# Routing on logits in PSUM, and places of rows summed by TensorE, in a macaron transformer block

## The chip, the cores and the metric

The kernel runs on one core of one Trainium2 chip. The metric is the device time of one execution in microseconds (us); it is the median of several executions. Engines: TensorE (PE, matmuls; PEld is its weight load), VectorE (DVE), ScalarE (ACT), GpSimd (POOL) and SyncE (SP, which issues DMAs). SBUF is the working memory; PSUM is eight banks that TensorE writes and VectorE and ScalarE read and write.

## The reference

The input x is 8 sequences of 512 rows of 128 values. The block applies a mixture of experts, then attention, then the same mixture of experts again:

```python
x = x + 0.5 * ffn(layernorm(x))          # 8 experts, 2 per row
x = x + attn(layernorm(x))               # 16 heads of 64, one shared K and V, causal, position bias
x = x + 0.5 * ffn(layernorm(x))

def ffn(x):
    gates = softmax(x @ gate_w)                    # 8 logits a row
    top_v, top_i = top_k(gates, 2)
    top_v = top_v / sum(top_v)
    h = gelu(einsum('nd,edf->enf', xt, fc_w))      # 128 -> 512
    eo = einsum('enf,efd->end', h, proj_w)         # 512 -> 128
    return sum(top_v * eo at top_i)                # the two chosen experts
```

## The kernel before

The 4096 rows are 32 tiles of 128. The kernel sends each row only to its two experts: it chooses the experts, gives each pair of row and expert a place in the list of that expert, scatters the rows there, and runs 71 tiles of sorted rows through the experts' matrices. This happens twice. The first expert stage runs from the start to about 250 us. The attention follows, to about 841 us. The second expert stage begins at about 865 us.

The routing of the second stage is woven into the attention. Its rows come in six groups of tiles (`GROUPS`: 8, 8, 8, 4, 2 and 2 tiles), as soon as the attention has finished them. A group is cut into pieces of up to four tiles (`PIECES`), so the first three groups have two pieces and the others one. The tasks of group i are:

- V2, A2, I2, X2: mean and deviation, and the normalised rows in `slot`.
- T2, C2, L2 (TensorE, ScalarE, TensorE), one for each piece: rows transposed, copied to SBUF, and multiplied with the gate; the logits stand in a PSUM bank, 8 columns a tile.
- G2 (VectorE, L1207), one for each piece: the logits are copied from the bank to `lga` in SBUF, and the bank is free.
- H2 (VectorE, L1217 to L1228), two halves, for the first and the second expert: the maximum, an `is_equal` with it, a product with `rev8` that favours the lower expert, a maximum, and an `is_equal` that leaves a one-hot `hot2`; the first half ends with the chosen logit masked in `lgb`, the second with `wt2` (L1226) and the sum of both one-hots, `hot2b` (L1227). `hot2_done` (L1228) follows.
- P2 (TensorE, L1505 and L1506): `hot2b` times all ones (rows of each tile by expert) and times `before` (rows ahead of this one in its tile), into one bank.
- W2 (ScalarE) and W3 (VectorE, L1231 to L1233): the weights.
- B2 (VectorE), two halves. The first (L1240 to L1250) runs a scan over tiles in `scan2` in SBUF, one step for each shift of 1, 2 and 4, adds the running counts `run`, and frees the bank by `base2_done`. The second (L1253 to L1255) picks each pair's place.
- SC (GpSimd, L795): the scatters.

The attention's own tasks, of batch b and step n (16 steps, 4 query tiles in each of 4 groups of heads): Q, K and V products; S, scores of four heads into two banks; TTR (VectorE, L1302), bias and maximum; EXP (ScalarE, L967); R (L1309) and N (GpSimd, L805), the normalisation, two instructions on SBUF each; T (TensorE, L1549) and TC (VectorE L1315 or ScalarE L974), transposed probabilities; AV, O, Y and YA (VectorE, L1324), the output.

All of these are put in order at build time by a list planner (`attention_order`). Each task has a cost, needs, a kind of bank that it takes and the task that frees this bank, and a due time (`wanted_at`); an engine takes the ready task that is due first. The engines then run their lists in that order, and wait on semaphores. There are four "front" banks for Q, K, V, xT, T2, L2, P2 and S; S takes two.

After the last group VectorE makes the lists of the second stage (`second_lists`), and SyncE loads sorted rows once all scatters have landed.

## Time and profile before

| | us |
|---|---|
| median of 3 runs | 1031.23 |
| lowest and highest | 1029.57, 1034.24 |
| profiled execution | 1030.17 |
| its span | 1028.4 |

| engine | busy us | share | instructions |
|---|---|---|---|
| PE | 936.7 | 91% | 7811 |
| PEld | 772.0 | 75% | 7811 |
| DVE | 763.2 | 74% | 2860 |
| ACT | 640.4 | 62% | 1765 |
| POOL | 637.2 | 62% | 613 |

How to read what follows. The profile records one execution. A timeline row gives start, duration, engine, source line, operation, the tile written and those read (buffer numbers left out, so `bank` is any PSUM bank), shapes, and in brackets how long the engine stood idle before it and what it waited for. A waits row gives who waited for whom: us in total, times, longest. A grouped row gives the busy time and the mean in ns. A windows row gives for one stretch its length, then busy time and instructions of PE, PEld, DVE, ACT and POOL, the granted TensorE clock as a share of 2.4 GHz, the DMA engines' share and GB/s.

### The profile page before, as it was taken

The numbers are of one execution on the slowest core, as the hardware profiler recorded it, in microseconds if no ns is written. First come the engines' busy times: TensorE is split into PE (matmuls) and PEld (weight loads), VectorE is DVE, ScalarE is ACT, GpSimd is POOL, SyncE is SP. The second block draws the span as 40 slices with busy tenths as digits, with TensorE's granted clock in tenths as the row PEclk, the third lists the DMA queues.
The fourth block names the chain that finished last, engine by engine and source line by source line (L and its number), as shares of the span: only waits on it lengthen the run. The fifth ranks groups of instructions, "written<-read, shape, count | busy, mean of one in ns | idle before, by whom it ended". The sixth has DMA issues, their size and how long they took to land.

```text
span 1028.4 us, 25473 instructions
## 1 busy us (share of the span) xinstructions
PE 936.7 (91%) x7811; PEld 772.0 (75%) x7811; DVE 763.2 (74%) x2860; ACT 640.4 (62%) x1765; POOL 637.2 (62%) x613
## 2 busy tenths in 40 slices
PE   8599999989999998899999899999899973999990
PEld 8499999957776777677776677777676753999990
DVE  7676456588788789877888877678978856777774
ACT  4735234488787888787888777788678651333330
POOL 2357577299889788788545587545586543555551
PEclk8699999999999999999999999999999995999996
DMA  9422556525556550010000000000010021222227
GB/s 270 132 65 68 91 128 150 107 61 127 133 104 135 119 109 15 19 33 2 2 2 1 12 33 2 2 2 1 12 33 1 5 88 54 74 68 72 71 58 245
DMA packets 86514, 69.57 MB, mean 68 GB/s; under 512 B 8034, under 2 KB 76388, under 8 KB 86384
## 3 DMA queue, kind: packets, MB, share of 16 engines
q1 hardware_dynamic: 77120, 48.92, 19.5%
q0 software_dynamic: 9264, 19.03, 7.3%
q8 instruction: 68, 1.11, 0.5%
q14 instruction: 62, 0.51, 0.2%
HBM read 32.07 MB, written 36.31 MB: 66 GB/s over the span
## 4 chain that ended last, share of the span: by engine, by line
PE 76%; DVE 9%; issue 4%; ACT 4%; DMA 3%; POOL 2%; SPq 1%; DVEq 0%; POOLq 0%; ACTq 0%
PE bank L1549 13%; PE bank L1540 13%; PE bank L1565 12%; PE bank L1601 12%; PE bank L1611 11%; PE bank L1572 6%; PE bank L1425 2%; PE bank L1427 2%; PE bank L1426 2%; PE bank L1593 2%; DMA xr<-xn_dram,gidx 1%; ACT prob L967 1%; DVE pT L1315 1%; DMA which<-y_dram 1%; DVE lnt L1044 1%
## 5 line engine op out<-in xcount | busy, mean ns | idle before, releaser
L805 POOL TENSOR_TENSOR prob<-prob,rsum 128x256 f32<-128x256 f32 (+3 forms) x256 | 314.0, 1254 | 138.4 <-DVE rsum L1309 137.7
L967 ACT ACTIVATE prob<-prob,negmax 128x384 f32<-128x384 f32 (+3 forms) x512 | 282.1, 553 | 66.9 <-DVE negmax L1302 66.2
L1302 DVE CUSTOM_DVE_ANT_0 prob<-bank,bias_tab 128x384 f32<-128x384 f32 (+3 forms) x512 | 229.1, 484 | 60.3 <-PE bank L1540 58.0
L904 ACT ACTIVATE hT<-bank 128x512 f32<-128x512 f32 x149 | 89.0, 597 | 205.9 <-PE bank L1601 205.9
L1549 PE MATMUL bank<-ident,prob 128*128 128x128 f32 x1280 | 186.5, 280 | 6.3 <-DVE pT L1315 5.2
L1540 PE MATMUL bank<-kst,qst 64*128 64x256 f32 (+2 forms) x1536 | 165.8, 343 | 14.0 <-DVE negmax L1302 7.6
L1549 PEld LDWEIGHTS bank<-ident,prob 128*128 128x128 f32 x1280 | 145.0, 142 | 39.4 <-issue 23.0
L1565 PE MATMUL bank<-pT,vst 128*64 128x256 f32 x1280 | 162.5, 389 | 1.3 <-DVE x_sb L1324 1.0
L1601 PE MATMUL bank<-xrT,w1t 128*128 128x128 f32 x1192 | 161.9, 280 | 1.0 <-DVE xrT L1360 0.9
L1540 PEld LDWEIGHTS bank<-kst,qst 64*128 64x128 f32 x1536 | 112.2, 186 | 62.5 <-issue 40.6
L1611 PE MATMUL bank<-w_sb,hT 128*128 x1192 | 158.7, 277 | 0.0
L1601 PEld LDWEIGHTS bank<-xrT,w1t 128*128 128x128 f32 x1192 | 148.5, 196 | 2.7 <-DVE xrT L1360 2.2
L1611 PEld LDWEIGHTS bank<-w_sb,hT 128*128 128x128 f32 x1192 | 146.5, 194 | 0.1
L1315 DVE COPY pT<-bank 128x512 f32<-128x512 f32 x181 | 123.6, 686 | 27.2 <-PE bank L1549 25.3
L818 POOL DMA_INDIRECT xr<-xn_dram,gidx x78 | 78.2, 1002 | 73.4 <-PE bank L1593 43.4
L1565 PEld LDWEIGHTS bank<-pT,vst 128*64 128x64 f32 x1280 | 82.8, 137 | 53.5 <-issue 20.1
L831 POOL DMA_INDIRECT y_dram<-yo,sidx x71 | 70.1, 987 | 75.2 <-DVE sidx L1358 68.2
L1372 DVE COPY w1t<-w_sb 128x512 f32 x149 | 66.4, 446 | 62.2 <-PE bank L1601 52.5
L967 ACT ACTIVATION_READ_ACCUMULATOR prob<-prob,negmax 128x1 f32 x512 | 96.8, 189 | 0.0
L974 ACT ACTIVATE pT<-bank 128x512 f32<-128x512 f32 x139 | 81.2, 588 | 24.9 <-PE bank L1549 24.1
L795 POOL DMA_INDIRECT slot_dram<-slot,idx x64 | 62.6, 979 | 35.0 <-DVE idx L1255 19.0
L1572 PE MATMUL bank<-wo_sb,ot 128*128 128x128 f32 x512 | 82.4, 288 | 1.8 <-ACT ot L980 1.7
(233 smaller groups left out, 1192.1 us busy)
## 6 DMA issues: line engine op xcount, KB each, us to landing
slot_dram<-fill SPq DMA_DIRECT2D x15, 990.0 KB, 7.2
y_dram<-yo SPq DMA_DIRECT2D x78, 64.0 KB
xr<-slot_dram SPq DMA_DIRECT2D x71, 66.0 KB, 1.8
w_sb<-L_ffn_fc_w SPq DMA_DIRECT2D x2, 2048.0 KB, 10.2
bias_tab<-bias_dram SPq DMA_DIRECT2D x8, 512.0 KB
slot_dram<-fill SPq DMA_DIRECT2D x2, 1056.0 KB, 7.5
x_sb<-L_attn_x SPq DMA_DIRECT2D x4, 512.0 KB, 5.6
xn_dram<-xn SPq DMA_DIRECT2D x4, 512.0 KB, 3.8
```

The lines of the kernel that those rows point to most:

```text
L805: g.tensor_tensor(out=pv, in0=pv, in1=rsum[:, n % 8, hs].unsqueeze(2).to_broadcast([P, 2, (n % QT + 1) * P]), op=ALU.mult).then_inc(norm_d ...
L904: a.activation(hT[:, n % 2, :], bank[2 + n % 2][:], ACT.Gelu).then_inc(gelu_done, 1)
L967: a.activation(prob[n % 8][:, h, :], prob[n % 8][:, h, :], ACT.Exp, scale=-1.0, bias=negmax[:, i % 8:i % 8 + 1], accum_out=lsum[:, n % 8, ...
L974: a.activation(pT[:, (b * NB + blk(n, jj)) % RING, :], BANK_OF["T", b, n, jj][:], ACT.Copy).then_inc(pt_act, 1)
L1302: v.tensor_tensor_reduce(out=prob[n % 8][:, h, :], in0=BANK_OF["S", b, n, c0][h % 2][:, at:at + w], in1=bias_tab[:, HG * (n // QT) + h, SE ...
L1315: v.tensor_copy(pT[:, (b * NB + blk(n, jj)) % RING, :], BANK_OF["T", b, n, jj][:]).then_inc(pt_dve, 1)
L1540: ins = t_.matmul(out[o][:, at:at + w], qst[rows, g % 2, zq, c, t * P:(t + 1) * P], kst[rows, b % 2, zk, 0:w], start=(i == 0), stop=(i == 2))
L1549: ins = t_.transpose(out[:, h * P:(h + 1) * P], prob[n % 8][:, h, jj * P:(jj + 1) * P], ident[:])
L1565: ins = t_.matmul(BACK_BANK[n % 2][o * DH:(o + 1) * DH, 0:2 * P], vst[:, b % 2, jj, :], heads, start=(jj == 0), stop=(jj == n % QT))
L1572: ins = t_.matmul(BACK_BANK[n % 2][:, 2 * P:2 * P + D], ot[:, n % 2, c * P:(c + 1) * P], wo_sb[:, n // QT, c, :], start=(c == 0), stop=(c ...
L1601: ins = t_.matmul(bank[2 + n % 2][:, c * P:(c + 1) * P], w1t[:, n % 2, c * P:(c + 1) * P], xrT[:, n % 2, :], start=True, stop=True)
L1611: ins = t_.matmul(bank[6 + n % 2][:, 0:D], hT[:, n % 2, c * P:(c + 1) * P], w2_sb[:, ds(e, 1), c, :].rearrange("p a d -> p (a d)"), start= ...
```

## The change

Three things.

- The last piece of each group has no G2. Its logits stay in their PSUM bank, at the place of their tile in the group, and the logits of an earlier piece are copied from `lga` into the same bank. `rev8` is copied there too. H2 works on these; the masked logits go to columns 128 and up of this bank, and `lgb` is gone. The bank is free when H2's second half is done.
- P2 multiplies `hot2b`, with one more tile of zeros behind it, with `before`, and adds for each tile q of the group one product with ones into the columns of all later tiles. The columns then hold the rows ahead of each row in the whole group, and the last tile's columns the group's totals. That is one matmul per tile and one more, where there were two.
- B2's first half is two additions (`run` to the bank's numbers, the totals to `run`), with its result in the bank. `scan2` and `base2_done` are gone. The bank is freed by B2's second half.

The planner's costs and the tasks that free the banks change with that, so the attention is put in order anew.

```diff
-                    task(("G2", m), {"dve": 0.2}, [("L2", m), ("H2", i - 1, 1)], None, ("L2", m))
-                task(("H2", i, 0), {"dve": 1.2}, [("G2", m) for m in mine] + [("B2", i - 1, 1), ("W3", i - 1)])
-                task(("H2", i, 1), {"dve": 1.6}, [("H2", i, 0)])
+                    if m != mine[-1]:
+                        task(("G2", m), {"dve": 0.2}, [("L2", m), ("H2", i - 1, 1)], None, ("L2", m))
+                task(("H2", i, 0), {"dve": 1.4}, [("G2", m) for m in mine[:-1]] + [("L2", mine[-1]), ("B2", i - 1, 1), ("W3", i - 1)])
+                task(("H2", i, 1), {"dve": 1.6}, [("H2", i, 0)], None, ("L2", mine[-1]))
...
-                task(("P2", i), {"pe": 0.3}, [("H2", i, 1)], "front")
-                task(("B2", i, 0), {"dve": 1.5}, [("P2", i)], None, ("P2", i))
-                task(("B2", i, 1), {"dve": 1.2}, [("B2", i, 0)])
+                task(("P2", i), {"pe": 0.3 + 0.1 * len(group)}, [("H2", i, 1)], "front")
+                task(("B2", i, 0), {"dve": 0.5}, [("P2", i)])
+                task(("B2", i, 1), {"dve": 1.2}, [("B2", i, 0)], None, ("P2", i))
...
                         if c == 0:
-                            dve.wait_ge(logit2_sb, max(LOGIT2_SB["G2", m] for m, piece in enumerate(PIECES) if piece[0] in group))
+                            if b == 0:
+                                async_done(v.memset(hot2b[:, 2 * QT, :], 0.0))
+                            dve.wait_ge(logit2_ps, LOGIT2_PS["L2", mine[-1]])
+                            if mine[:-1]:
+                                dve.wait_ge(logit2_sb, max(LOGIT2_SB["G2", m] for m in mine[:-1]))
+                                ahead_of_last = slice(js.start, js.start + sum(len(PIECES[m]) for m in mine[:-1]))
+                                async_done(v.tensor_copy(room[:, 0:(ahead_of_last.stop - js.start) * E], lga[:, ahead_of_last, :].rearrange("p t e -> p (t e)")))
+                            step_done(v.tensor_copy(room[:, 2 * QT * E:2 * QT * E + E], rev8[:]))
...
-                        rev = rev8[:].unsqueeze(1).to_broadcast([P, nt, E])
-                        src = (lga, lgb)[c]
+                        rev = room[:, 2 * QT * E:2 * QT * E + E].unsqueeze(1).to_broadcast([P, nt, E])
+                        src = (logits, rest)[c]
...
-                            step_done(v.scalar_tensor_tensor(out=lgb[:, js, :], in0=hot2[:, 0, js, :], scalar=MASKED, in1=lga[:, js, :],
+                            step_done(v.scalar_tensor_tensor(out=rest, in0=hot2[:, 0, js, :], scalar=MASKED, in1=logits,
                                                              op0=ALU.mult, op1=ALU.add))
...
                             dve.wait_ge(prefix2_ps, b + 1)
-                            async_done(v.memset(scan2[:, :, 0:4, :], 0.0))
-                            async_done(v.tensor_copy(scan2[:, 0, 4, :], run[:]))
-                            step_done(v.tensor_copy(scan2[:, 0, 5:4 + nt, :], tot[:, 0:nt - 1, :]))
-                            cur = 0
-                            for sh in [x for x in (1, 2, 4) if x < nt]:
-                                step_done(v.tensor_tensor(scan2[:, 1 - cur, 4:4 + nt, :], scan2[:, cur, 4:4 + nt, :],
-                                                          scan2[:, cur, 4 - sh:4 + nt - sh, :], ALU.add))
-                                cur = 1 - cur
-                            async_done(v.tensor_tensor(run[:], scan2[:, cur, 3 + nt, :], tot[:, nt - 1, :], ALU.add))
-                            step_done(v.tensor_tensor(lgb[:, js, :], scan2[:, cur, 4:4 + nt, :], pre, ALU.add))
-                            v.engine_nop().then_inc(base2_done, 1)
+                            step_done(v.tensor_tensor(place2, rows_ahead, run[:].unsqueeze(1).to_broadcast([P, nt, E]), ALU.add))
+                            async_done(v.tensor_tensor(run[:], sums[:, nt * E:(nt + 1) * E], run[:], ALU.add))
...
-                                step_done(v.tensor_tensor(eqa[:, js, :], lgb[:, js, :], hot2[:, c, js, :], ALU.mult))
+                                step_done(v.tensor_tensor(eqa[:, js, :], place2, hot2[:, c, js, :], ALU.mult))
...
-                        hot = hot2b[:, slots_of(GROUPS[b]), :].rearrange("p t e -> p (t e)")
-                        t_.matmul(out[:, 0:nt * E], ones_bf[:], hot, start=True, stop=True)
-                        t_.matmul(out[:, 2 * QT * E:(2 * QT + nt) * E], before[:], hot, start=True, stop=True).then_inc(prefix2_ps, 1)
+                        hot = hot2b[:, 2 * QT - nt:2 * QT + 1, :]
+                        t_.matmul(out[:, 0:(nt + 1) * E], before[:], hot.rearrange("p t e -> p (t e)"), start=True, stop=False)
+                        for q in range(nt):
+                            ins = t_.matmul(out[:, (q + 1) * E:(nt + 1) * E], ones_bf[:], hot[:, q:q + 1, :].to_broadcast([P, nt - q, E]),
+                                            start=False, stop=(q == nt - 1))
+                        ins.then_inc(prefix2_ps, 1)
```

## Rows read from the trace of the kernel before

**Rows 1.** The page, busy time: engine, us, share of the span, instructions.
```profile
PE 936.7 (91%) x7811; PEld 772.0 (75%) x7811; DVE 763.2 (74%) x2860; ACT 640.4 (62%) x1765; POOL 637.2 (62%) x613
```

**Rows 2.** Busy time by stretch: attention with routing, then the handover to the experts.
```profile
250.00:836.00 586.00, 564.40 (x4639) 419.82 (x4641) 468.19 (x1677) 459.42 (x1351) 410.68 (x364) 0.99 0.16 37
836.00:865.20 29.20, 7.75 (x52) 5.23 (x48) 18.70 (x100) 8.02 (x15) 9.14 (x9) 0.65 0.29 98
```

**Rows 3.** Waits of TensorE from 245 to 845 us: us in total, times, longest.
```profile
PE bank L1540 <- DVE negmax L1302: 5.8, 4, 2.6
...
PE bank L1540 <- DVEq L1250: 2.8, 2, 1.4
...
PE bank L1505 <- DVEq L1228: 2.6, 1, 2.6
```

**Rows 4.** Timeline, H2 of group 0: start, us, engine, instruction, idle before it.
```profile
412.73 3.74 POOL L805 TENSOR_TENSOR prob<-prob,rsum 128x1024 f32<-128x1024 f32 x2 [1.47 <-DVE rsum L1309]
...
412.79 1.92 DVE L1218 TENSOR_TENSOR eqa<-lgb,top 128x64 f32<-128x64 f32 x1
...
414.74 1.82 DVE L1219 TENSOR_TENSOR eqa<-eqa,rev 128x64 f32<-128x64 f32 x1
...
417.61 0.19 PE L1505 MATMUL bank<-hot2b,ones_bf 128*128 128x64 bf16 x1 [2.58 <-DVEq L1228]
```

**Rows 5.** Timeline, an instruction with one input in a bank beside GpSimd's.
```profile
423.42 2.04 POOL L805 TENSOR_TENSOR prob<-prob,rsum 128x512 f32<-128x512 f32 x2 [1.69 <-DVE rsum L1309]
...
424.18 0.68 DVE L1281 TENSOR_TENSOR xTl<-bank,xTh 128x512 fp32r<-128x512 f32 x1
```

**Rows 6.** Groups of VectorE instructions by shape: busy us, mean ns, idle before.
```profile
L1253 DVE TENSOR_TENSOR eqa<-lgb,hot 128x64 f32<-128x64 f32 x6 | 3.4, 562 | 0.1
...
L1221 DVE TENSOR_TENSOR hot<-rev,slot 128x64 f32<-128x64 f32 x3 | 0.7, 226 | 0.1
...
L1245 DVE TENSOR_TENSOR scan<-scan 128x16 f32<-128x16 f32 x2 | 0.3, 174 | 0.1
...
L1249 DVE TENSOR_TENSOR lgb<-scan,bank 128x16 f32<-128x16 f32 x2 | 0.3, 162 | 0.0
```

**Rows 7.** Timeline, the sums of group 1 and the S behind them.
```profile
574.48 0.11 DVE L1240 MEMSET scan<- 128x64 f32 x1
...
574.76 1.35 DVE L1245 TENSOR_TENSOR scan<-scan 128x64 f32<-128x64 f32 x3
...
576.23 0.21 DVE L1249 TENSOR_TENSOR lgb<-scan,bank 128x64 f32<-128x64 f32 x1
...
576.64 0.79 PE L1540 MATMUL bank<-kst,qst 64*128 64x384 f32 x6 [1.41 <-DVEq L1250]
```

**Rows 8.** Timeline, the sums of group 3 and the AV behind them.
```profile
815.65 0.58 DVE L1241 COPY scan<-run 128x8 f32<-128x8 f32 x1
...
817.61 1.08 PE L1565 MATMUL bank<-pT,vst 128*64 128x256 f32 x8 [0.98 <-DVE x_sb L1324]
```

**Rows 9.** Timeline, eight bf16 matmuls in a row in the first routing.
```profile
29.47 0.45 PE L1480 MATMUL bank<-which,in_tile 128*128 128x40 bf16 x8 [3.79 <-DVE in_tile L1131]
```

**Rows 10.** Busy time by stretch, behind P2's wait in group 0; clock third from last.
```profile
418.30:421.70 3.40, 3.40 (x18) 2.87 (x17) 2.44 (x14) 2.66 (x10) 2.94 (x4) 0.50 0.07 19
421.70:425.10 3.40, 3.40 (x29) 2.55 (x28) 3.13 (x15) 2.06 (x6) 1.71 (x3) 1.00 0.09 24
```

**Rows 11.** Timeline of the handover: sums of group 5, scatters, first expert tile.
```profile
853.89 0.11 DVE L1240 MEMSET scan<- 128x64 f32 x1
...
854.67 0.17 DVE L1253 TENSOR_TENSOR eqa<-lgb,hot 128x16 f32<-128x16 f32 x1
...
855.94 0.96 POOL L795 DMA_INDIRECT slot_dram<-slot,idx  x1 [1.79 <-DVE idx L1255]
...
865.22 0.48 PE L1593 MATMUL bank<-ident,xr 128*128 128x128 f32 x1 [11.78 <-DMA xr<-slot_dram]
```

**Rows 12.** Timeline, G2 of group 0's last piece, then the S that takes its bank.
```profile
405.98 0.19 DVE L1207 COPY lga<-bank 128x32 f32<-128x32 f32 x1
...
407.81 0.96 PE L1540 MATMUL bank<-kst,qst 64*128 64x512 f32 x6
```

32 lines of the change are left out of this document (20 added, 12 removed).

## The prediction

> **What bounds the kernel now.** I read the busy line first, then busy time by stage, then TensorE's waits, then the timeline around each wait that bears on the changed code. The page gives TensorE 91% of the span [rows 1]. By stage [rows 2]: from 250 to 836 us, the attention with the second routing woven in, TensorE is busy 564.40 of 586.00 us, so 21.6 us of idleness is all that a faster VectorE could hand back there; VectorE is busy 468.19, so it has 118 us of slack. From 836.0 to 865.2 TensorE has next to nothing to do: that is a chain of small steps, and each step that goes shortens the run. From 865.2 on the experts run, and the change touches nothing there. So the change can act on (1) those TensorE waits of the attention that the routing causes, (2) the chain at the handover, (3) TensorE's own work.
>
> Of (1), the waits show three kinds [rows 3]: P2 waited 2.6 us once for `hot2_done` (L1228), S waited 2.8 us in two places for `base2_done` (L1250, the bank of the sums), and S waited 5.8 us for L1302, the ordinary traffic of the attention.
>
> Why the routing is late is seen at group 0 [rows 4]. GpSimd's normalisation (L805, two instructions in 3.74 us) starts at 412.73. VectorE's L1218 starts at 412.79 and takes 1.92 us, L1219 then 1.82 us, each ending just as one GpSimd instruction ends. The same shape undisturbed takes about 0.23 us (L1221 in [rows 6]), so 1.92 + 1.82 - 0.45 = 3.3 us are waiting, and P2 left TensorE idle for 2.58 us. What waits has two inputs in SBUF. With one in PSUM it does not: L1281, started at 424.18 under GpSimd's instructions of 423.42 to 425.46, took its usual 0.68 us [rows 5].
>
> The Trainium skill says the same (SBUF: State Buffer, section Who interferes with whom): a VectorE instruction with two SBUF inputs is blocked by a GpSimd one that reads SBUF, whichever starts second. By that rule L1226 (two slices of `top2`) and L1227 (two slices of `hot2`) stay exposed after the change; that is rival B.
>
> **The change part by part**, against the profiled execution's 1030.17 us.
>
> *H2, group 0.* L1217 to L1223 get a PSUM input or have one SBUF input already; only the chain of L1226 and L1227 can still wait. Without the 3.3 us, `hot2_done` comes before P2's place in TensorE's order, and 2.58 us go; if GpSimd's second instruction holds L1227 instead, some 1 us goes; if both positions fall badly, nothing. I take -1.7, ends 0 and -2.6. Right behind this gap TensorE ran at 1.2 GHz for 3.40 us [rows 10], starting 18 matmuls there against 29 in the next 3.40 us at 2.4 GHz: 3.4 x (1 - 18/29) = 1.3 us lost. If the idleness before it shrinks, this may go too: -0.6, ends 0 and -1.3.
>
> *B2, groups 1 and 2* (one wait for L1250 each, 2.8 us in all [rows 3]). The sums start at 574.48; three scan steps take 1.35 us, two of them behind GpSimd, and S waited 1.41 us for the bank until 576.64 [rows 7]. The change leaves two instructions (0.21 + 0.08, with 0.03 to 0.04 between: about 0.33 us) but hands the bank back only after B2's second half, five instructions at about 0.25 us, 1.2 us. That is 1.5 us where there were 1.96 (574.48 to 576.44, the end of L1249): the wait shrinks by 0.5 us, not by 1.4. -1.0 for both, ends 0 and -2.8. B2's second half gains too: six L1253 took 562 ns on average, against 226 for the shape undisturbed (L1221), 2.0 us in all [rows 6], and S waits for VectorE 5.8 us in the stage [rows 3]. I let 0.6 come through, ends 0 and -2.0.
>
> *B2, group 3.* L1241 stood 0.58 us behind GpSimd, and YA, next on VectorE behind the sums, let TensorE wait 0.98 us [rows 8]. The sums lose L1241 and all scan steps: -0.8, ends 0 and -1.0.
>
> *The handover.* Group 5, two tiles. G2 goes (0.17), the copy of `rev8` comes (0.17): nothing. The sums start at 853.89 and B2's second half at 854.67: 0.78 us, now 0.21 + 0.08 = 0.3. W3 still sets their start. GpSimd's last four scatters waited for exactly this index (idle 1.79 until 855.94), TensorE for what follows from them [rows 11]. Group 4's same saving is swallowed by the wait for group 5. So -0.46. Not shown by any row is a VectorE write into PSUM. The chain now has two of them per group (the `rev8` copy and the masked logits), four in all, each from the 0.17 us of the same write to SBUF to 0.23 us, the largest undisturbed VectorE row of this code; I take 0.17, since reads of PSUM are no dearer here: with one input in the bank L1249 takes 162 ns where L1245, both in SBUF, takes 174 [rows 6].
>
> A rule speaks against this step: the Trainium skill (VectorE: DVE Perf Modes, section on the TRN2 errata) puts the fixed part of a PSUM-source operation at 120 cycles against 58 from SBUF at 0.96 GHz, 65 ns more. Twenty operations on the handover's chain change their source (nine in each H2, two in B2), so its estimate is +1.3 us, and -0.46 would turn into +0.8. The 162 against 174 ns above contradict it, and I leave it out.
>
> *P2.* One matmul per tile and one more, where there were two: 7 more in three groups, 3 in one, 1 in two, 26 in all. Eight bf16 matmuls of 128x40 in a row took 0.45 us [rows 9]; with one at about 0.19 the next seven come 0.037 us apart. 26 x 0.037 = +0.96 us, nearly all in the full stage. Ends 0 (they fit into waits) and +2.6 (0.1 us each, the cost that the new listing gives its planner).
>
> *New holds.* The last L2 of a group now keeps one of the four front banks until H2 is through, and S needs two. By the order that the planner writes for the kernel before, in group 0 the copy at 405.98 freed the bank for the S at 407.81 [rows 12]; H2 ended only at 417.4 [rows 4]. In group 3 a Q took it at once. In groups 1 and 2 its taker, an S, started after the time at which H2 ended anyway: nothing. VectorE's waits on GpSimd that vanish shorten the hold, and transposes and AV fill TensorE meanwhile: I take +0.8 for groups 0 and 3 together, ends 0 and the slow rival. The remaining additions (the copy of `lga`, `rev8`, one memset, some 2 us in all) lie in VectorE's 118 us of slack.
>
> Sum: -1.7 - 0.6 - 1.0 - 0.6 - 0.8 - 0.46 + 0.96 + 0.8 = -3.4, or 1026.8. The median of the runs, 1031.23, stands 1.06 above the profiled execution, and I carry that over: 1027.8 us.
>
> **The rivals.**
>
> A, *everything comes back*: all terms at their good ends but P2's, -2.6 - 1.3 - 2.8 - 2.0 - 1.0 - 0.46 + 0.96 = -9.2, 1022.0 us. For it: every gap named ends at an instruction of the routing. Against: 21.6 us is the whole idleness, and the bank is handed back later.
>
> B, *the wait moves*: L1226, L1227 and W3 still read SBUF alone, GpSimd is busy 410.68 of 586 us [rows 2], and an H2 that runs faster to its end meets the instruction it used to outwait. Then only the sums are shorter, against 0.96 for P2: about 1031 us.
>
> C, *slower, by the held bank*: S in groups 0 and 3 cannot take its two banks until H2 is done, H2 is queued behind VectorE's other work because it is due later, and TensorE runs dry. Price: the largest wait of S in the attention is 2.6 us [rows 3]; with 1.3 us of lower clock behind it, 3.9, in two groups 7.8; with P2's 0.96 and half of the gains that remain left over, 1031.2 + 7.8 + 1.0 - 2.0 = 1038 us. It decides once H2 needs longer from the last L2 than S can be put off, in more than one group. Against: groups 1 and 2 pay nothing. For: since the order is planned anew, every later task shifts as well, and which of them meet a GpSimd instruction is drawn again; that shift has no sign and is in the width of the range.
>
> **How the numbers follow.** Forecast 0.45, with a range of its own from 1024.5 to 1031; A 0.17; B 0.20; C 0.18. About 0.5% (5.2 us) is what a measurement of this kernel can tell from no change: faster is below 1026.1, slower above 1036.4. Faster: A and a third of the forecast, 0.32. Slower: C, 0.18. Same: 0.50. The range takes in all but C: 1021.5 to 1035.5.
>
> **What would show it.** Right, if L1218, L1219 and L1253 of the new kernel take their 0.23 us under GpSimd's instructions; if P2 no longer waits; if the handover from the last L2 to the last scatter is 0.5 us shorter; if TensorE's idleness in the attention falls by 3 to 5 us and its work grows by 1. B shows as long instances of the wt and hot2b lines; C as new waits of S or Q for H2's last step. I am wrong if the new order of the attention moves more than the routing does: then gaps appear at L1302 and L1549, far from H2.

## The result, and the profile of the changed kernel

| | before | after |
|---|---|---|
| median, us | 1032.74 | 1019.04 |
| profiled execution, us | 1030.17 | 1018.65 |
| its span, us | 1028.4 | 1016.7 |

The changed kernel takes 0.9872 of the time before, with an interval of 0.9853 to 0.9891: 13 us faster. That is below the whole range of 1021.5 to 1035.5, and below the 1022.0 of the rival in which everything comes back. The direction was right, the size was not. The ratio leaves out one of the changed kernel's four executions, which took 1862.64 us; the others took 1018.47 to 1019.43.

The page after, busy time; it answers [rows 1].

```profile
PE 935.8 (92%) x7837; PEld 772.6 (76%) x7837; DVE 747.7 (74%) x2834; ACT 640.3 (63%) x1764; POOL 638.2 (63%) x613
```

TensorE has 26 instructions more, as the step on P2 counted, and the same busy time; VectorE has 15.5 us less. So nearly all of the time came out of idleness. Where, the busy time by stretch tells: around the batches that carry groups 0, 1 and 2, then nearly the whole attention with routing. First the kernel before (columns as in [rows 2]).

```profile
370.00:455.00 85.00, 79.43 (x649) 59.38 (x647) 72.20 (x257) 66.09 (x193) 67.17 (x63) 0.98 0.19 45
530.00:612.00 82.00, 77.55 (x633) 57.11 (x631) 67.27 (x236) 64.36 (x189) 50.84 (x46) 1.00 0.04 14
686.00:768.00 82.00, 77.54 (x637) 57.39 (x633) 67.86 (x240) 62.56 (x184) 50.87 (x45) 1.00 0.04 13
245.00:829.00 584.00, 562.40 (x4627) 417.98 (x4627) 468.85 (x1683) 460.83 (x1353) 409.30 (x363) 0.99 0.16 37
```

The same stretches of the changed kernel.

```profile
370.00:455.00 85.00, 81.83 (x689) 61.18 (x685) 69.68 (x263) 68.46 (x199) 70.19 (x66) 0.98 0.20 48
530.00:612.00 82.00, 80.33 (x671) 60.18 (x670) 66.34 (x247) 66.50 (x200) 56.28 (x50) 1.00 0.05 15
686.00:768.00 82.00, 80.35 (x673) 60.11 (x674) 66.15 (x242) 66.01 (x191) 55.94 (x50) 1.00 0.05 15
245.00:829.00 584.00, 571.60 (x4745) 426.56 (x4745) 461.58 (x1689) 467.02 (x1363) 416.82 (x369) 0.99 0.16 37
```

TensorE's idleness from 245 to 829 us falls from 584 - 562.40 = 21.6 us to 12.4. Each of the three stretches gives 2.4 to 2.8 us of it (2.40, 2.78, 2.81). The attention itself, from its first AV to its last, takes 614.7 us where it took 626.2: 11.5 us, the whole difference of the two profiled executions.

What TensorE still waits for in that stretch (columns as in [rows 3]).

```profile
PE bank L1561 <- DVE pT L1322: 5.6, 4, 1.4
PE bank L1552 <- DVE qst L1296: 2.8, 1, 2.8
PE bank L1552 <- DVE negmax L1309: 2.6, 1, 2.6
PE bank L1577 <- DVE x_sb L1331: 0.6, 3, 0.2
```

Of the routing's waits in [rows 3] none is left: `hot2_done` and `base2_done` are gone and no wait for H2's last step has taken their place. What B2 still causes is small: 0.2 us of an S that waits for a bank of the sums (`idx`, L1262, in group 3), and the 0.6 us of AV. (Lines have moved: S is L1552, T L1561, AV L1577, TTR L1309, TC L1322, YA L1331, GpSimd's normalisation L809.) H2 of group 0, which answers [rows 4]:

```profile
408.73 2.89 POOL L809 TENSOR_TENSOR prob<-prob,rsum 128x768 f32<-128x768 f32 x2 [1.49 <-DVE rsum L1316]
...
409.28 0.22 DVE L1234 TENSOR_TENSOR eqa<-bank,top 128x64 f32<-128x64 f32 x1
...
409.54 0.22 DVE L1235 TENSOR_TENSOR eqa<-eqa,bank 128x64 f32<-128x64 f32 x1
...
413.93 0.22 DVE L1243 TENSOR_TENSOR hot2b<-hot 128x64 bf16<-128x64 f32 x1
...
417.99 0.20 PE L1514 MATMUL bank<-hot2b,before 128*128 128x72 bf16 x1
```

These two steps are of H2's first half, and they take 0.22 us under GpSimd's normalisation. The steps of [rows 4] that took 1.92 and 1.82 us are of the second half. In the changed kernel that half runs at 412.57, when GpSimd issues gathers (`DMA_INDIRECT`, 411.77 to 416.51) and no normalisation is under way, so this group alone does not show what the bank did for it. The fair comparison is the first half with the same order of tasks and its operands in SBUF (`e13_sbuf_operands`, see the experiments):

```profile
408.09 2.89 POOL L810 TENSOR_TENSOR prob<-prob,rsum 128x768 f32<-128x768 f32 x2 [1.49 <-DVE rsum L1317]
...
408.57 1.07 DVE L1235 TENSOR_TENSOR eqa<-lga,top 128x64 f32<-128x64 f32 x1
...
409.67 1.39 DVE L1236 TENSOR_TENSOR eqa<-eqa,rev 128x64 f32<-128x64 f32 x1
...
412.71 0.96 PE L1553 MATMUL bank<-kst,qst 64*128 64x512 f32 x6 [1.25 <-DVE qst L1297]
```

1.07 and 1.39 us there, 0.22 and 0.22 with an operand in the bank, and TensorE's wait of 1.25 us for `qst`, the task behind them, is gone. Over the whole trace it is as clear. Take VectorE's two-input instructions of at most 64 columns that begin while a GpSimd `tensor_tensor` has 0.3 us or more still to run. In the kernel before there are 28, all with both inputs in SBUF, and all 28 take longer than 0.3 us. In the changed kernel the 12 with both in SBUF do, and the 18 with one in a bank do not.

In the changed kernel `hot2b` ends at 414.15, P2 comes in its turn at 417.99, and nothing waits. The sums of group 1, which answer [rows 7]:

```profile
569.03 6.89 POOL L809 TENSOR_TENSOR prob<-prob,rsum 128x1024 f32<-128x1024 f32 x6 [5.46 <-DVE rsum L1316]
...
573.29 0.22 DVE L1256 TENSOR_TENSOR bank<-bank,run 128x64 f32<-128x64 f32 x1
573.55 0.17 DVE L1257 TENSOR_TENSOR run<-bank,run 128x8 f32<-128x8 f32 x1
...
574.71 0.24 DVE L1262 CAST idx<-posa 128x16 int32<-128x16 f32 x1
...
575.76 1.08 PE L1577 MATMUL bank<-pT,vst 128*64 128x256 f32 x8 [0.20 <-DVE x_sb L1331]
```

All seven instructions of B2 are done in 1.66 us (573.29 to 574.95) below a GpSimd chain, where the first half alone took 1.96 and the second another 1.94. TensorE loses 0.20 us to what follows them.

The handover, which answers [rows 11].

```profile
843.18 0.17 DVE L1256 TENSOR_TENSOR bank<-bank,run 128x16 f32<-128x16 f32 x1
...
843.47 0.16 DVE L1260 TENSOR_TENSOR eqa<-bank,hot 128x16 f32<-128x16 f32 x1
...
844.73 0.96 POOL L799 DMA_INDIRECT slot_dram<-slot,idx  x1 [1.83 <-DVE idx L1262]
...
853.98 0.48 PE L1605 MATMUL bank<-ident,xr 128*128 128x128 f32 x1 [11.34 <-DMA xr<-slot_dram]
```

The sums take 0.29 us (843.18 to 843.47) where they took 0.78. From the last group of AV products to this first matmul of the experts it is 853.98 - 827.49 = 26.49 us, against 865.22 - 838.26 = 26.96 before: 0.47 us shorter.

### The profile page after: what moved, and what is told of

The parts are those of the page before. It is cut to its first block, busy times and chain, and to the rows that moved or that the text cites. A ratio compares the mean times of both kernels' runs of the same rounds, so it can differ in the third digit from the quotient of the medians.

```text
span 1016.7 us, 25497 instructions
## 1 busy us (share of the span) xinstructions
PE 935.8 (92%) x7837; PEld 772.6 (76%) x7837; DVE 747.7 (74%) x2834; ACT 640.3 (63%) x1764; POOL 638.2 (63%) x613
## 4 chain that ended last, share of the span: by engine, by line
PE 79%; DVE 8%; issue 4%; ACT 3%; DMA 3%; POOL 2%; SPq 1%; DVEq 0%; POOLq 0%; ACTq 0%
PE bank L1561 13%; PE bank L1552 13%; PE bank L1577 13%; PE bank L1613 12%; PE bank L1623 12%; PE bank L1584 6%; PE bank L1432 2%; PE bank L1434 2%; PE bank L1433 2%; ACT prob L971 2%; PE bank L1605 2%; DMA xr<-xn_dram,gidx 1%; DMA which<-y_dram 1%; DVE lnt L1048 1%; PE bank L1508 1%
## 5 line engine op out<-in xcount | busy, mean ns | idle before, releaser
L809 POOL TENSOR_TENSOR prob<-prob,rsum 128x256 f32<-128x256 f32 (+3 forms) x256 | 314.1, 1255 | 129.7 <-DVE rsum L1316 129.1
L1309 DVE CUSTOM_DVE_ANT_0 prob<-bank,bias_tab 128x384 f32<-128x384 f32 (+3 forms) x512 | 229.8, 484 | 64.5 <-PE bank L1552 61.8
L1561 PE MATMUL bank<-ident,prob 128*128 128x128 f32 x1280 | 184.0, 279 | 6.6 <-DVE pT L1322 5.6
L1552 PE MATMUL bank<-kst,qst 64*128 64x256 f32 (+2 forms) x1536 | 165.9, 343 | 7.9 <-DVE negmax L1309 4.5
L1561 PEld LDWEIGHTS bank<-ident,prob 128*128 128x128 f32 x1280 | 144.3, 142 | 37.0 <-issue 19.7
L1577 PE MATMUL bank<-pT,vst 128*64 128x256 f32 x1280 | 163.0, 390 | 0.8 <-DVE x_sb L1331 0.6
L1552 PEld LDWEIGHTS bank<-kst,qst 64*128 64x128 f32 x1536 | 112.6, 187 | 56.1 <-issue 38.8
L1322 DVE COPY pT<-bank 128x512 f32<-128x512 f32 x182 | 124.3, 686 | 27.2 <-PE bank L1561 25.6
L1577 PEld LDWEIGHTS bank<-pT,vst 128*64 128x64 f32 x1280 | 83.4, 137 | 52.8 <-issue 20.9
```

Source lines behind the costliest of these rows:

```text
L809: g.tensor_tensor(out=pv, in0=pv, in1=rsum[:, n % 8, hs].unsqueeze(2).to_broadcast([P, 2, (n % QT + 1) * P]), op=ALU.mult).then_inc(norm_d ...
L1309: v.tensor_tensor_reduce(out=prob[n % 8][:, h, :], in0=BANK_OF["S", b, n, c0][h % 2][:, at:at + w], in1=bias_tab[:, HG * (n // QT) + h, SE ...
L1322: v.tensor_copy(pT[:, (b * NB + blk(n, jj)) % RING, :], BANK_OF["T", b, n, jj][:]).then_inc(pt_dve, 1)
L1552: ins = t_.matmul(out[o][:, at:at + w], qst[rows, g % 2, zq, c, t * P:(t + 1) * P], kst[rows, b % 2, zk, 0:w], start=(i == 0), stop=(i == 2))
L1561: ins = t_.transpose(out[:, h * P:(h + 1) * P], prob[n % 8][:, h, jj * P:(jj + 1) * P], ident[:])
L1577: ins = t_.matmul(BACK_BANK[n % 2][o * DH:(o + 1) * DH, 0:2 * P], vst[:, b % 2, jj, :], heads, start=(jj == 0), stop=(jj == n % QT))
```

## The experiments

Two things for reading them. The chips differ: on two of them the kernel before took 1077 and 1089 us, on the others 1031 to 1033, so each ratio is against the kernel before on the same chip, and absolute times are compared on one chip alone. And "choice" is H2, "sums" is P2 with B2's first half, "place" is the tile that the second half of B2 reads.

### The whole change again, and one part alone, each with an order of its own

`e8_changed_again` and `e16_changed_third` are the changed kernel itself, beside the other experiments of their chip.

> The changed kernel itself, timed beside the others. The first four experiments ran on a chip on which the kernel before took 1077 us instead of 1032, so the changed kernel is needed as a reference on the same chip. If its gain does not depend on the chip: 12 to 14 us below the kernel before, a ratio of 0.987.

> The changed kernel, as reference for the other three on their chip. On a chip on which the kernel before takes 1032 us: 1018 us. On one on which it takes 1077 to 1089 us, where TensorE waits twice as long in the attention for other reasons: a ratio between 0.984 and 0.99.

Measured: 0.986 (0.9842 to 0.9877) and 0.9892 (0.9873 to 0.9911). The three ratios of the change, 0.9872 among them, scatter by 0.3%; differences below that between experiments on different chips say nothing.

`e1_sbuf_operands` and `e9_sbuf_operands`: the changed kernel with its order, P2 and B2, but with every operand back in SBUF.

```diff
-                        logits, rest = of_group(0), of_group(4 * QT * E)
+                        logits, rest = lga[:, js, :], lgb[:, js, :]
...
-                        rev = room[:, 2 * QT * E:2 * QT * E + E].unsqueeze(1).to_broadcast([P, nt, E])
+                        rev = rev8[:].unsqueeze(1).to_broadcast([P, nt, E])
...
-                        place2 = sums[:, 4 * QT * E:(4 * QT + nt) * E].rearrange("p (t e) -> p t e", e=E)
+                        place2 = lgb[:, js, :]
```

> The changed kernel with the same order of tasks on every engine, but the choice of experts works on copies in SBUF (lga, lgb, rev8) and the places are summed into SBUF. One copy per group (rev8) is left out. Only where the operands stand differs from the changed kernel. Theory 1 (the gain is VectorE no longer waiting for GpSimd): L1218, L1219 and L1253 of the old numbering are held again in some places, each by 0.8 to 1.9 us, and TensorE's gaps behind H2 and B2 come back: 5 to 9 us slower than the changed kernel, 1024 to 1028 us. Theory 2 (the gain is the newly planned order): within 1.5 us of the changed kernel, 1018 to 1020.5 us. Theory 3 (the gain is the shorter sums): within 1.5 us as well, since the sums keep their two instructions.

> The kernel of e1 once more (the changed kernel with its operands back in SBUF, order unchanged), now to be compared with the changed kernel's 1018.1 us and with the order-only kernel's 1033.2 us on a chip like theirs. Theory 1 (waits on GpSimd): between 1026 and 1029 us, with some VectorE instructions held 0.8 to 1.9 us. Theory 3 (shorter sums): at most 1020 us.

`e2_choice_only` and `e10_choice_only` have the new H2 with the old P2 and B2 (scan, `base2_done`), put in order anew (against the changed kernel):

```diff
-                task(("P2", i), {"pe": 0.3 + 0.1 * len(group)}, [("H2", i, 1)], "front")
-                task(("B2", i, 0), {"dve": 0.5}, [("P2", i)])
-                task(("B2", i, 1), {"dve": 1.2}, [("B2", i, 0)], None, ("P2", i))
+                task(("P2", i), {"pe": 0.3}, [("H2", i, 1)], "front")
+                task(("B2", i, 0), {"dve": 1.5}, [("P2", i)], None, ("P2", i))
+                task(("B2", i, 1), {"dve": 1.2}, [("B2", i, 0)])
```

> Only the first part of the change: the choice works in the bank of the logits, the bank is held until H2 is through; P2 and the scan in B2 are those of before. Theory 1: H2 no longer waits, P2's 2.6 us in group 0 and what follows go, but the scan steps of groups 1 and 2 can still be held: 1024 to 1028 us. Theory 2: unforeseeable, as the order is planned anew with other costs, 1018 to 1034 us. Theory 3: no gain, 1030 to 1034 us.

> The kernel of e2 once more (the choice in the bank, P2 and B2 as before). From e2's ratio of 0.998: 1029 us. If the choice alone gives the larger part on a chip without the other chip's additional waits: 1024 us.

`e3_places_only` and `e11_places_only` have the new P2 and B2 with the old H2 and G2, put in order anew (against the changed kernel):

```diff
-                    if m != mine[-1]:
-                        task(("G2", m), {"dve": 0.2}, [("L2", m), ("H2", i - 1, 1)], None, ("L2", m))
+                    task(("G2", m), {"dve": 0.2}, [("L2", m), ("H2", i - 1, 1)], None, ("L2", m))
```

> Only the second part of the change: TensorE sums the tiles ahead, B2 has two additions into the bank, and the bank is freed at B2's end; H2, G2 and their bank are those of before. Theory 3: the gaps of 1.4 us in groups 1 and 2 and of 1.0 in group 3 go, and 0.5 us at the handover: 1024 to 1027 us. Theory 1: half of the gain, since the product with the one-hots reads the bank now, but H2 is held as before with P2 behind it: 1026 to 1030 us.

> The kernel of e3 once more (the places in the bank and summed by TensorE, the choice as before). From e3's ratio of 0.9945: 1026 us. If choice and places add up to the whole 13.6 us: this one and e10 lie 13.6 us below twice the time before when taken together.

| | chip at 1077.11 | chip at 1089.47 |
|---|---|---|
| operands in SBUF | 0.9955 (0.9937 to 0.9973) | 0.9915 (0.9877 to 0.9953) |
| choice only | 0.9977 (0.996 to 0.9994) | 0.996 (0.9933 to 0.9987) |
| sums and place only | 0.9945 (0.9929 to 0.9962) | 0.9944 (0.9919 to 0.997) |

The kernel before took the times at the head of the table. Each part alone gains, the sums with the place about 0.55%, the choice 0.2 to 0.4%. Together that is 0.8 to 1%, under the 1.1 to 1.4% of the whole. But each had an order of its own, and the whole was not run on these two chips, so these runs cannot tell whether the parts help each other. Hence the third set.

### The held bank

`e4_held_bank` and `e12_held_bank`: the kernel before, with only the planner told that the last L2's bank is held until H2 is done, and the semaphores to match.

```diff
-                    task(("G2", m), {"dve": 0.2}, [("L2", m), ("H2", i - 1, 1)], None, ("L2", m))
+                    task(("G2", m), {"dve": 0.2}, [("L2", m), ("H2", i - 1, 1)], None, ("L2", m) if m != mine[-1] else None)
...
-                task(("H2", i, 1), {"dve": 1.6}, [("H2", i, 0)])
+                task(("H2", i, 1), {"dve": 1.6}, [("H2", i, 0)], None, ("L2", mine[-1]))
```

> The kernel before with one difference in the plan: the bank of the last logits of a group is freed by H2's second half instead of by the copy G2. No instruction differs, only the order and who waits for the bank. If the held bank costs what the prediction took: 0.8 us slower than before. Rival C of the prediction: up to 8 us slower. If it is free: no difference beyond 0.5 us, unless the order that is planned anew changes which VectorE instructions meet a GpSimd instruction, which by theory 2 can move the time by several us either way.

> The kernel of e4 once more (the kernel before, with the last logits' bank planned as held to the end of H2). From e4's ratio of 1.006: 1038 us. If its loss was a matter of the other chip: within 2 us of the kernel before. If the hold itself costs, TensorE's new gaps stand before an S or a Q that waits for H2; if it is the order planned anew, they stand elsewhere, behind VectorE instructions held by GpSimd.

Measured: 1.0063 (1.0046 to 1.008) and 1.002 (0.9991 to 1.005). A loss of 0.6% on the one chip, not to be told from nothing on the other. It doesn't come as the rival said. TensorE's waits in `e4_held_bank` show none for H2, one routing wait only, that for `base2_done` (L1252 here, 2.8 us in [rows 3]):

```profile
PE bank L1542 <- DVEq L1252: 4.5, 3, 1.6
```

The sums and the places have grown instead. Groups of VectorE instructions in `e4_held_bank`, columns as in [rows 6]:

```profile
L1247 DVE TENSOR_TENSOR scan<-scan 128x64 f32<-128x64 f32 x9 | 5.7, 632 | 0.3
L1255 DVE TENSOR_TENSOR eqa<-lgb,hot 128x64 f32<-128x64 f32 x6 | 4.6, 767 | 0.1
```

The scan steps took 360 ns on average before, the places 562 [rows 6]. In the new order the same instructions fall behind more of GpSimd's, while those of H2's second half, held before, are not. So the held bank itself shows no price; what changed is the order. That this order is what lost the 2 to 7 us (by the two ratios) is not shown: the kernel before has no trace on these two chips to set beside it.

### The same order for all: which part does it

These four run TensorE, VectorE, ScalarE and GpSimd in the order of the changed kernel; only the operands and instructions within the tasks differ. `e5_order_only` puts the old H2, P2 and B2 into it, with all operands in SBUF as in the first diff and the old sums:

```diff
-                            step_done(v.tensor_tensor(place2, rows_ahead, run[:].unsqueeze(1).to_broadcast([P, nt, E]), ALU.add))
-                            async_done(v.tensor_tensor(run[:], sums[:, nt * E:(nt + 1) * E], run[:], ALU.add))
+                            async_done(v.memset(scan2[:, :, 0:4, :], 0.0))
+                            async_done(v.tensor_copy(scan2[:, 0, 4, :], run[:]))
...
+                            step_done(v.tensor_tensor(lgb[:, js, :], scan2[:, cur, 4:4 + nt, :], pre, ALU.add))
```

> The order of tasks on every engine and the freeing of banks as in the changed kernel, but the instructions of the kernel before: the choice and the places in SBUF, the scan on VectorE, two products in P2. Theory 2 (the newly planned order gives the gain): within 2 us of the changed kernel. Theory 1 and theory 3 together (the instructions give it): at least as slow as the kernel before, ratio 0.998 to 1.005, since the planner also reckons with a B2 that is 1 us shorter than it is here. Compared with e1 (ratio 0.9955) it gives the worth of the shorter sums in one and the same order: theory 3 expects 2 to 4 us between them.

`e14_choice_in_bank_same_order` has the new H2 with those old sums.

> The order of the changed kernel and its choice in the bank, but P2 with two products and the scan in SBUF of the kernel before. Against e5 it has only the choice's operands moved. In the trace of e5 H2 was held 4.2 us in all and B2 4.4: 3 to 6 us faster than e5 and 8 to 11 us slower than the changed kernel.

`e13_sbuf_operands` has the new sums with all operands in SBUF (the first diff above).

> The order of the changed kernel, its P2 and its two additions in B2, but every operand of the choice and of the places in SBUF (as e1 and e9). If waiting on GpSimd is what costs: 8 to 10 us slower than the changed kernel, as in its trace 8.0 us of such waits stood in H2 and B2. If the shorter sums are what counts: within 2 us of the changed kernel.

`e15_places_in_sbuf` has everything but the place, which stands in SBUF:

```diff
-                        place2 = sums[:, 4 * QT * E:(4 * QT + nt) * E].rearrange("p (t e) -> p t e", e=E)
+                        place2 = lgb[:, js, :]
```

> The changed kernel with one operand elsewhere: the sum of rows ahead and run is written to SBUF instead of the bank, so that only the two products with the one-hots in B2's second half can wait for GpSimd. Such products were held 3 to 4 us in all in e13's order. If every us held here delays the bank for S: 3 to 5 us slower than the changed kernel; if they stand beside other work: within 1 us.

| in the order of the changed kernel | choice | sums | place | ratio | attention | idle | at 1.2 GHz |
|---|---|---|---|---|---|---|---|
| order only | SBUF | old | SBUF | 1.0015 (1.0 to 1.003) | 627.2 | 23.2 | 12.5 |
| choice in bank | bank | old | SBUF | 1.0006 (0.9989 to 1.0023) | 627.8 | 20.2 | 22.9 |
| operands in SBUF | SBUF | new | SBUF | 0.9949 (0.9929 to 0.9969) | 619.8 | 17.9 | 8.6 |
| place in SBUF | bank | new | SBUF | 0.9906 (0.9884 to 0.9928) | 616.7 | 15.0 | 9.2 |
| changed, same chip | bank | new | bank | 0.9892 (0.9873 to 0.9911) | 615.3 | 12.4 | 12.0 |

The last three columns are us of the traced execution, from the first AV to the last: its length, TensorE's idleness, and the time at 1.2 GHz. All but the first ran on one chip.

The new order brings nothing in time, if anything it costs 1.5 us. By time, the choice in a bank is worth 0.1% while the sums are long (across two chips, and below the 0.3% that says nothing there) and 0.4% (4.7 us) once they are short. The short sums are worth 0.7% with the choice in SBUF (across two chips again) and 1.1% (1032.28 to 1020.9, 11.4 us) with it in a bank. The place in a bank adds 0.9 us, less than the intervals. Operands in SBUF came out 5.5 us above the changed kernel, where 8 to 10 were expected if only the holds counted, and choice in bank 1.0 us below order only (across two chips), where 3 to 6 were.

By idleness the parts simply add up. The choice takes away 3.0 us with long sums and 2.9 with short ones, the short sums 5.3 and 5.2, the place 2.6. If there is more between the parts than that, it lies in the clock, see below.

What the sums and the place shorten is one wait of TensorE, that of AV for YA (`x_sb`). It stands, in this sequence, in the order only, choice in bank, operands in SBUF and place in SBUF kernels, from 245 to 829 us:

```profile
PE bank L1582 <- DVE x_sb L1339: 6.8, 3, 2.8
```
```profile
PE bank L1582 <- DVE x_sb L1339: 7.0, 3, 2.8
```
```profile
PE bank L1578 <- DVE x_sb L1332: 2.3, 2, 1.1
```
```profile
PE bank L1578 <- DVE x_sb L1332: 2.6, 3, 1.2
```

In the changed kernel it is the 0.6 us shown above. The choice does not touch it (6.8 and 7.0, 2.3 and 2.6 us). In the new order YA is queued on VectorE behind both halves of B2, so the whole of B2 now stands between TensorE and its next AV. In the choice in bank kernel, group 1:

```profile
576.68 0.11 DVE L1256 MEMSET scan<- 128x64 f32 x1
...
579.13 0.80 DVE L1268 TENSOR_TENSOR eqa<-lgb,hot 128x64 f32<-128x64 f32 x1
...
581.27 0.47 DVE L1339 TENSOR_TENSOR x_sb<-x_sb,bank 128x128 f32<-128x128 f32 x2
581.69 1.98 PE L1582 MATMUL bank<-pT,vst 128*64 128x256 f32 x8 [2.82 <-DVE x_sb L1339]
```

From the first instruction of B2 to YA it is 4.59 us here, 2.05 in the changed kernel (573.29 to 575.34). In the choice in bank kernel less idleness goes with more time at the lower clock. The first three stretches of the table above, in the choice in bank kernel:

```profile
370.00:455.00 85.00, 80.95 (x657) 60.32 (x656) 70.64 (x263) 68.33 (x198) 69.01 (x64) 0.98 0.21 48
530.00:612.00 82.00, 77.69 (x628) 58.07 (x625) 64.90 (x239) 62.94 (x188) 49.72 (x44) 0.96 0.04 13
686.00:768.00 82.00, 77.68 (x637) 58.26 (x636) 65.82 (x241) 61.98 (x184) 49.91 (x44) 0.98 0.04 13
```

A granted clock of 0.96 and 0.98 where the kernel before has 1.00: TensorE ran at 1.2 GHz for 22.9 us of the attention in all, against 12.5 in the order only kernel. It is idle 3.0 us less, but busy 3.6 us longer (627.8 - 20.2 against 627.2 - 23.2), and so the attention takes as long. The traced execution is no exception: over all ten the mean granted clock is 0.952 of full speed, against 0.955 over the ten of order only. Why more time at 1.2 GHz came with the shorter choice, no run shows.

What the place in SBUF costs is seen one instruction at a time. The operands in SBUF kernel, group 1, below GpSimd instructions from 570.96 to 577.84:

```profile
576.22 0.71 DVE L1261 TENSOR_TENSOR eqa<-lgb,hot 128x64 f32<-128x64 f32 x1
...
577.22 0.66 DVE L1263 CAST idx<-posa 128x16 int32<-128x16 f32 x1
...
578.69 1.08 PE L1578 MATMUL bank<-pT,vst 128*64 128x256 f32 x8 [1.12 <-DVE x_sb L1332]
```

Two instructions there are held for 0.5 us each. In the changed kernel the first reads a bank. The cast, the same instruction in both, took 0.24 us there, below GpSimd's chain too; why it escaped, no row shows.

### More products in P2

`e7_more_products`: the changed kernel with 32 more products of ones with the zero tile. They add nothing to the sums.

```diff
+                        for q in range(nt):
+                            ins = t_.matmul(out[:, (q + 1) * E:(nt + 1) * E], ones_bf[:], hot[:, nt:nt + 1, :].to_broadcast([P, nt - q, E]),
+                                            start=False, stop=(q == nt - 1))
```

> The changed kernel with one more product per tile in P2, of ones with the tile of zeros, 32 in all; same order, same result. It prices P2's matmuls in place. The prediction took 0.037 us for each: 1.2 us slower than the changed kernel. If they fit into waits: no difference (below 0.5 us). If each costs 0.1 us: 3.2 us slower.

Measured: 1019.86 us against 1018.07 for the changed kernel on the same chip, 1.8 us for 32, 0.056 us each; for the 26 of the change, 1.5 us. The intervals of the two overlap (0.9861 to 0.9895 and 0.9842 to 0.9877), so this is a rough size. The timeline has less for them, eight in 0.21 us (420.35 to 420.56):

```profile
420.35 0.35 PE L1516 MATMUL bank<-hot2b,ones_bf 128*128 128x64 bf16 x8
...
420.56 0.35 PE L1519 MATMUL bank<-hot2b,ones_bf 128*128 128x64 bf16 x8
```

That would be 0.026 us each, 0.8 us for 32. The other 1.0 us is small beside the scatter, and whether the products delay something else is open.

### The gaps that are left: the deviation

TensorE's six waits above 1 us that the changed kernel keeps (11.0 us in all, nearly all of the list of waits above) stand behind LN or I2, the tasks that compute the deviation. One of the largest, in the timeline:

```profile
331.09 4.27 DVE L1282 SCALAR_TENSOR_TENSOR shift<-mv,rstd 128x4 f32<-128x4 f32 x1
...
331.58 3.75 POOL L809 TENSOR_TENSOR prob<-prob,rsum 128x1024 f32<-128x1024 f32 x2
...
336.60 0.79 PE L1552 MATMUL bank<-kst,qst 64*128 64x384 f32 x6 [2.62 <-DVE negmax L1309]
```

An instruction on four columns, 0.16 us when it is alone, is held until 335.36, as GpSimd's two end at 335.33, and TensorE idles 2.62 us. `e6_deviation_in_bank` is the changed kernel with one operand of each of these steps in a PSUM bank (LN and I2 take a front bank for it, so the order is planned anew):

```diff
-                task(("LN", b), {"dve": 1.0}, [("LA", b)])
+                task(("LN", b), {"dve": 1.2}, [("LA", b)], "front", ("LN", b))
...
+                y, z = BANK_OF[k][:, 0:n], BANK_OF[k][:, 64:64 + n]
+                step_done(v.reciprocal(y, lnt[:, 4, own]))
+                async_done(v.scalar_tensor_tensor(out=z, in0=mean[:, own], scalar=-1.0, in1=y, op0=ALU.mult, op1=ALU.mult))
+                step_done(v.scalar_tensor_tensor(out=lnt[:, 0, own], in0=var[:, own], scalar=EPS, in1=y, op0=ALU.add, op1=ALU.mult))
+                step_done(v.scalar_tensor_tensor(out=lnt[:, 1, own], in0=lnt[:, 0, own], scalar=-0.5, in1=y, op0=ALU.mult, op1=ALU.mult))
```

> The changed kernel, and the same idea carried on to the deviations (LN and I2): the reciprocal, and the mean times it, are written to a front bank, so that L1043 to L1045 and the shift have one input there and one in SBUF. One small instruction more each time; the planner gives LN and I2 a front bank for their 1.2 us. Theory 1: in the changed kernel six of the seven remaining gaps of TensorE over 1 us in the attention (2.6, 2.8 and four of 1.3 to 1.5 us) stand behind such an instruction, 9.8 us in all; with the stretches at 1.2 GHz behind two of them, 5 to 11 us faster than the changed kernel. If the waits on GpSimd were not what counts, or the order planned anew decides: no gain, or 3 us slower.

Measured: 1007.96 us, 0.9769 (0.9749 to 0.9788) of the kernel before, 10.1 us under the changed kernel on the same chip. It beats both. The groups of VectorE instructions, one line of the changed kernel and the one that answers it:

```profile
L1048 DVE SCALAR_TENSOR_TENSOR lnt<-lnt 128x8 f32<-128x8 f32 x3 | 4.2, 1392 | 0.1
```
```profile
L1069 DVE SCALAR_TENSOR_TENSOR lnt<-lnt,bank 128x8 f32<-128x8 f32 x3 | 0.5, 162 | 0.1
```

1392 ns become 162. In this kernel 45 small VectorE instructions with one input in a bank begin under a GpSimd `tensor_tensor`, by the count above, and none is held. TensorE's idleness in the attention falls from 12.4 to 3.1 us, and no stretch of it is at 1.2 GHz. The attention is 19.3 us shorter (595.4 against 614.7 us), but it starts later: the first AV comes at 222.4 instead of 214.4 us. How much of either is the new order, and how much the operands, was not taken apart.

## Why the prediction was wrong

*The bound and the mechanism: right.* It named 21.6 us of idleness as all that could come back, and found the reason, VectorE instructions with two SBUF inputs held behind GpSimd's. The Trainium skill (SBUF — State Buffer, Who interferes with whom) says so, and the trace agrees: 28 of 28 such instructions held before, 12 of 12 after, and none of the 18 with an input in a bank. Of H2, B2 and W3, 20 instructions in the attention took longer than a third of a microsecond before (16.5 us lost) and 5 after (4.3 us).

*H2, group 0: -1.7 taken, -2.40 measured in its stretch, but not for the reason given.* The term said that P2's 2.58 us go because H2's operands stand in a bank. They go without that: in the order only kernel, with H2 in SBUF, the second half meets no normalisation, its steps take 0.22 us, and P2 waits 0.20 us. That was luck in the order. The stretch from 370 to 455 us gained nothing by it, for the first half is held there instead (1.06 and 1.39 us) and S waits 1.25 us for the `qst` behind it: TensorE is idle 5.6 us in it before, 5.6 in order only, 4.0 with the choice in a bank, 3.2 in the changed kernel. The bank took 1.6 us of that away and the short sums 0.9. The term came near the 2.40 by luck.

*B2, groups 1 and 2: the step that failed.* -1.0 was taken for both waits for the bank, with -0.6 for B2's second half. The two stretches gained 2.78 and 2.81, 5.6 us against 1.6. In group 1 the wait for the bank gave 1.41 us of it, three gaps of 0.5 us each (see the rivals) 1.60, and AV's new wait took 0.20. The reasoning was that the bank comes back after 1.5 us instead of 1.96, so a wait of 1.4 us shrinks by 0.5. The 1.5 was nearly right (1.66 measured). Wrong was to keep its other end fixed: the S that waited for this bank takes another one in the new order, and what stands behind B2 is YA. In the new order the length that counted was B2 as a whole up to YA, and that fell from 4.59 us with the old sums to 2.05. The order alone made things worse: in the order only kernel AV waits 2.8 us there in each of the two groups, where S had waited 1.4. In group 1's stretch TensorE is idle 4.4 us before, 4.9 in order only, 1.7 in the changed kernel. The choice behind GpSimd in these groups, which delayed the maximum of the scores, was in no term: S waits for `negmax` 4.1 us in three places in the operands in SBUF kernel, and 2.8 us in one in place in SBUF, which differs from it in the choice alone.

*B2, group 3: -0.8 taken.* Of the 0.98 us of [rows 8] 0.18 is left, with 0.17 of an S behind it. The batch around it also lost 0.6 us of another gap (2.05 before, 1.43 after) and the stretch at 1.2 GHz behind it. That gap's own cause is I2, which is held as before (1.47 and 1.39 us in both kernels, under GpSimd instructions of 2.89 and 2.90 us); another task stands behind it in the new order. Order only has it at 1.42 us too. Not a gain of the routing, but of the draw.

*Lower clock: -0.6 taken, 0 in the sum.* The stretch behind P2's wait did go [rows 10], and that of batch 7, but others came. Before, and then after:

```profile
786.90:790.30 3.40, 3.40 (x20) 2.63 (x20) 2.27 (x6) 3.20 (x9) 0.00 (x0) 0.50 0.00 0
```
```profile
211.00:218.00 7.00, 6.26 (x23) 3.50 (x23) 4.07 (x12) 5.11 (x16) 6.51 (x8) 0.51 0.11 28
...
392.05:395.45 3.40, 3.40 (x22) 2.44 (x22) 2.23 (x12) 3.40 (x14) 2.80 (x3) 0.50 0.02 7
```

The one at 392 follows a gap of 2.76 us that both kernels have, and only in the changed one the clock fell behind it. In sum 10.2 us before and after's 10.4 (counted within the attention). A single gap does not fix whether the clock falls.

*P2: +0.96 taken, 1.5 by the experiment.* Within its ends, and no better known than the overlap of the two intervals allows.

*The handover: -0.46 taken, -0.47 measured.* The one chain without slack, worked out from undisturbed rows. The dearer PSUM source of the Trainium skill (VectorE: DVE Perf Modes, section on the TRN2 errata) would have made it +0.8; the trace contradicts it again, with the -0.47 and with 0.22 us for L1234 and L1235, which read a bank, against 226 ns for the same shape from SBUF [rows 6]. The write into a bank, unknown then, now has rows: 229 ns with 64 columns (the masked logits), where the write to SBUF took 224, and 164 ns for `rev8`.

*The held bank: +0.8 taken, nothing found.* No wait for H2 in the attention of the changed kernel; the order as a whole, held banks and all, came out 1.5 us above the kernel before, with an interval from 0 to 0.3% (order only).

*The rivals.* The wait did not move to L1226 and L1227: none of them was held. W3 was, 3.6 us in three instructions, where five had lost 6.1 us before; TensorE shows at most AV's 0.2 us behind each of them. The slower case had the right point, that the order is drawn anew, and the held bank kernel that lost 0.6% fits it. (Its price was read a little low: the largest wait of S was 2.8 us, for `qst`, not 2.6.) "Everything comes back" had the right mechanism but stopped at the gaps that could be laid to a routing instruction in the waits. Gaps of 0.5 us put down to `pT`, `ot` and `negmax` around the sums (569.6, 578.5 and 582.9 us, and the same three in group 2) went too, 3.2 us in all; in the order only kernel those at `pT` and `ot` are gone as well, so these are the order's. They were counted as the ordinary traffic of the attention.

Of the 11.5 us, the idleness of the attention (22.6 to 12.4 us) explains 10.2. With P2's extra work the rest is some 2.8 us that no row here accounts for.

What failed, then, was not the mechanism but the size of one term: B2 in groups 1 and 2 was put at 1.6 us and gave 5.6. The measured wait for the bank was shortened by half of itself only, and the gaps of 0.5 us beside it stood in no term. The other terms were put below their bounds as well, and 0.8 us was added for a held bank that no run shows a wait for. The forecast of -3.4 us had its own good end at -9.2, and the truth was beyond it; 2.8 us of that stay unexplained.

## What to carry to other kernels

Where VectorE and GpSimd both work from SBUF, look for small VectorE instructions that take more than twice the time of their shape, and put one operand of each in PSUM: with shorter sums that gave 13 us in the routing, and 10 more in the deviation (the order planned anew in both). When such an instruction stands before others in an engine's list, its price is the whole task's length up to what TensorE next needs, not the wait for its own semaphore; read what is queued behind it. When a change makes a planner order everything anew, run the new order with the old instructions too: here it had already removed the gap that looked like the first gain, and put others in its place. And add up idleness, not time: the idleness of the parts added up to within 0.1 us, while their times did not, as the time at the lower clock differed from kernel to kernel.

## What the runs showed of the hardware that was not expected

A held instruction can lose more than one GpSimd instruction: L1282 was held over two of them, 4.27 us for 0.16 us of work. Its record begins 0.49 us before the first of theirs, while GpSimd still issued a gather; the starts on GpSimd are rough, and why it was not through by then is open.

GpSimd's `DMA_INDIRECT` does not hold them as its `tensor_tensor` does. Of VectorE's small instructions with two SBUF inputs that begin under one, with 0.3 us or more of it still to run, 34 of 35 take their usual time in the kernel before and 32 of 33 in the changed one. The exception in both is the instruction just named (L1275 before).

One SBUF input can be enough. L1247, a `tensor_scalar` of 8 columns from SBUF to SBUF, took 1.33 us below GpSimd's chain. The cast shown above took 0.66 us, and the copy of [rows 8] 0.58:

```profile
571.47 1.33 DVE L1247 TENSOR_SCALAR wt<-wt 128x8 f32<-128x8 f32 x1
```

The Trainium skill (SBUF — State Buffer, Who interferes with whom) has this too, copy, cast and `tensor_scalar` being able to take the shared port pair; the trace agrees for these three, and shows none of the reductions of H2 and B2 held (0.22 us each under GpSimd's chain).

The same kernel took 1031 to 1033 us on some chips and 1077 or 1089 us on two others. The operands in SBUF kernel was traced on three of them. Single instructions have the same durations (GpSimd's normalisation of 1024 columns 1894 to 1896 ns, the copy of `pT` 686); but the attention takes 652.6 and 654.7 us on the slower two against 619.8, with TensorE idle for 40.5 and 42.0 us against 17.9, and 25.7 and 24.5 us at 1.2 GHz against 8.6. What sets that off was not looked into.
